# Layer-norm statistics of a four-layer graph kernel: two rows read by one statistics instruction

## The reference

```python
def _layernorm(x, axis=-1, eps=1e-05):
    m = jnp.mean(x, axis=axis, keepdims=True)
    v = jnp.var(x, axis=axis, keepdims=True)
    return (x - m) / jnp.sqrt(v + eps)

x = _layernorm(x + _L0_gnn_ref(...), axis=-1)
x = _layernorm(x + _L1_gnn_ref(...), axis=-1)
x = _layernorm(x + _L2_gnn_ref(...), axis=-1)
x = _layernorm(x + _L3_gnn_ref(...), axis=-1)
```

## Time and profile before

| | |
|---|---|
| median of 3 runs | 1827.29 us (1821.63 to 1827.8) |
| the profiled execution | 1824.94 us |
| its span, first to last instruction | 1822.8 us |
| PE, DVE, ACT, POOL busy | 1447.3, 1518.1, 1085.2, 1221.6 us |
| mean granted clock of TensorE | 0.923 |
| statistics instructions (L660) | 1,800, of 276 to 281 ns |

### The profile page before, as it was taken

One profiled execution on the slowest core, in us unless ns is written; L12 is line 12 of the kernel. 1 busy time (PEld: TensorE's weight loads), 2 busy tenths in 40 slices (PEclk: granted clock), 3 DMA queues, 4 the chain that ended last, 5 costly groups with the idle time before them and its releaser, 6 DMA issues.

```text
span 1822.8 us, 24302 instructions
## 1 busy us (share of the span) xinstructions
PE 1447.3 (79%) x6228; PEld 920.3 (50%) x6228; DVE 1518.1 (83%) x4392; ACT 1085.2 (60%) x2688; POOL 1221.6 (67%) x910
## 2 busy tenths in 40 slices
PE   2677777777787737877888499999898499999995
PEld 1344444444454425666666355555555255555552
DVE  3999999999999947999999589999999366666663
ACT  0467777777777754999999735655555233333331
POOL 7467666666766737888883188877772557777764
PEclk8789989899989878999999789999999799999998
DMA  5334444444444335676675445455442333443320
GB/s 145 84 79 100 100 105 105 93 101 97 96 107 105 62 94 126 180 189 181 187 189 159 126 111 128 124 132 138 130 107 76 100 88 88 98 98 90 88 75 21
DMA packets 165804, 205.15 MB, mean 113 GB/s; under 512 B 66823, under 2 KB 97918, under 8 KB 165666
## 3 DMA queue, kind: packets, MB, share of 16 engines
q1 hardware_dynamic: 108066, 179.45, 37.3%
q0 software_dynamic: 57600, 24.15, 7.5%
HBM read 147.12 MB, written 70.80 MB: 120 GB/s over the span
## 4 chain that ended last, share of the span: by engine, by line
DVE 59%; PE 27%; issue 8%; ACT 3%; DMA 1%; SPq 1%; POOL 0%; DVEq 0%; POOLq 0%; ACTq 0%
PE po L1210 16%; DVE bst L660 16%; DVE masked L866 5%; DVE run L738 5%; DVE po L707 4%; DVE sel L709 4%; DVE y L703 3%; DVE po L706 3%; DVE y L698 2%; PE pt L1195 2%; PE po L1205 2%; PE pb L1433 2%; PE pa L1474 1%; PE pc L1474 1%; PE pb L1474 1%
## 5 line engine op out<-in xcount | busy, mean ns | idle before, releaser
L475 POOL DMA_INDIRECT xs<-target_rows,slot_all x276 | 385.7, 1397 | 235.4 <-DMA xs<-source_rows 156.1
L951 ACT ACTIVATE x<-y,nmr,rst 125x128 f32<-125x128 f32 x800 | 322.7, 481 | 47.5 <-DVE nmr L688 47.5
L1210 PE MATMUL po<-wnt,rt 128*125 128x384 f32 x800 | 311.6, 538 | 0.6 <-ACT rt L988 0.6
L475 POOL DMA_INDIRECT xs<-in_x,src_all x100 | 148.1, 1481 | 136.2 <-issue 136.2
L1210 PEld LDWEIGHTS po<-wnt,rt 128*125 128x125 f32 x800 | 172.9, 216 | 117.0 <-issue 40.2
L1205 PE MATMUL po<-ball,ones_bf 128*125 128x512 bf16 (+1 forms) x512 | 153.2, 429 | 80.5 <-DVE sel L709 76.5
L1195 PE MATMUL pt<-ident,x 125*128 125x125 f32 x800 | 125.1, 280 | 99.5 <-issue 73.1
L1210 PE MATMUL po<-wnt,run 128*125 128x384 f32 x600 | 201.5, 486 | 0.0
L482 POOL DMA_INDIRECT out_rows<-do,last_all x100 | 121.5, 1215 | 89.9 <-ACT do L951 48.4
L660 DVE BATCH_NORM_STATS2 bst<-y 125x6 f32<-125x128 f32 x800 | 164.8, 278 | 3.8
L951 ACT ACTIVATE do<-yd,nmr,rst 125x128 f32<-125x128 f32 x400 | 163.6, 482 | 6.6 <-DVE nmr L688 6.6
(11 more groups left out here) (188 smaller groups left out, 3150.0 us busy)
## 6 DMA issues: line engine op xcount, KB each, us to landing
xin<-in_x SPq DMA_DIRECT2D x100, 224.0 KB
out_rows<-res SPq DMA_DIRECT2D x100, 224.0 KB
same<-same_d SPq DMA_DIRECT2D x75, 250.0 KB, 4.0
source_rows<-so SPq DMA_DIRECT2D x75, 224.0 KB
target_rows<-do SPq DMA_DIRECT2D x75, 224.0 KB
xs<-source_rows SPq DMA_DIRECT2D x69, 224.0 KB
xd<-target_rows SPq DMA_DIRECT2D x59, 224.0 KB
rel<-in_etype SPq DMA_DIRECT2D x50, 250.0 KB, 4.7
```

Source lines behind the costliest of these rows:

```text
L475: return nc.gpsimd.indirect_dma_start(out=to, out_offset=None, in_=table, in_offset=bass.IndirectOffsetOnAxis(ap=index, axis=0), bounds_ch ...
L951: last = A(to[:, j, :], y[:, j, :], ACT.Identity, scale=rst[s][:, k:k + 1], bias=nmr[s][:, k:k + 1])
L1210: last = mm(po[0:R, j * 512:j * 512 + NT * D], left(j), wnt[:, k, :, :].rearrange("k t d -> k (t d)"), start=False, stop=stop, skip_group_ ...
```

## The change

A statistics instruction now reads two rows of a partition at once, with their elements alternating: element 0 of row j, element 0 of row j+1, element 1 of row j, and so on, 256 elements. Its even half is then row j and its odd half is row j+1, each complete, so the sums that joined halves are left out. The table of statistics has three numbers a row, where it had six. The epsilon terms are added by operations with two tensor inputs, the second a constant held in memory (floors), and the copy in edge_rows1 is written as a maximum of a tensor with itself. The mean is read from the table with its own stride.

```diff
-        bst = two(sb, "bst", [R, G * T, 6])
-        msum, mdif, ve, seed, rst, nmr, tmp = (two(sb, n, [R, G * T]) for n in
-                                                   ("msum", "mdif", "ve", "seed", "rst", "nmr", "tmp"))
+        bst = two(sb, "bst", [R, G * T, 3])
+        floors = sb("floors", [R, 2])
+        ve, seed, rst, nmr, tmp = (two(sb, n, [R, G * T]) for n in ("ve", "seed", "rst", "nmr", "tmp"))
...
+            V.memset(floors[:, 0:1], D * EPS * EPS)
+            V.memset(floors[:, 1:2], D * EPS)
...
             def stats(y, s, g):
-                for j in range(T):
-                    last = V.bn_stats(bst[s][:, g * T + j, :], y[:, j, :])
+                for j in range(0, T, 2):
+                    to = bst[s][:, g * T + j:g * T + j + 2, :].rearrange("p j k -> p (j k)")
+                    last = V.bn_stats(to, y[:, j:j + 2, :].rearrange("p j d -> p d j"))
                 return last
 
             def variances(s, n, twice):
-                g, both = slice(0, n * T), twice * T
-                b_, ms, md, v, q = (a[s] for a in (bst, msum, mdif, ve, tmp))
-                V.tensor_tensor(md[:, g], b_[:, g, 1], b_[:, g, 4], ALU.subtract)
-                V.tensor_tensor(ms[:, g], b_[:, g, 1], b_[:, g, 4], ALU.add)
-                step(V.tensor_tensor(v[:, g], b_[:, g, 2], b_[:, g, 5], ALU.add))
-                step(V.scalar_tensor_tensor(out=q[:, g], in0=md[:, g], scalar=D / 4.0, in1=md[:, g], op0=ALU.mult, op1=ALU.mult))
-                step(V.tensor_tensor(v[:, g], v[:, g], q[:, g], ALU.add))
+                both = twice * T
+                v, m2 = ve[s], bst[s][:, :, 2]
                 if twice:
-                    last = V.tensor_scalar(v[:, 0:both], v[:, 0:both], 1.0 + EPS, D * EPS * EPS, ALU.mult, ALU.add)
+                    last = V.scalar_tensor_tensor(out=v[:, 0:both], in0=m2[:, 0:both], scalar=1.0 + EPS,
+                                                  in1=floors[:, 0:1].broadcast_to([R, both]), op0=ALU.mult, op1=ALU.add)
                 if n > twice:
-                    last = V.tensor_scalar(v[:, both:n * T], v[:, both:n * T], D * EPS, None, ALU.add)
+                    last = V.tensor_tensor(v[:, both:n * T], m2[:, both:n * T],
+                                           floors[:, 1:2].broadcast_to([R, n * T - both]), ALU.add)
                 last.then_inc(s_var, 1)
...
-                V.scalar_tensor_tensor(out=m[:, g], in0=ms[:, g], scalar=-0.5, in1=r[:, g],
+                V.scalar_tensor_tensor(out=m[:, g], in0=b_[:, g, 1], scalar=-1.0, in1=r[:, g],
                                        op0=ALU.mult, op1=ALU.mult).then_inc(done, 1)
...
-                return V.tensor_copy(bst[s][:, T:2 * T, :], bst[s][:, 4 * T:5 * T, :])
+                edge = bst[s][:, 4 * T:5 * T, :]
+                return V.tensor_tensor(bst[s][:, T:2 * T, :], edge, edge, ALU.max)
```

More of the change, by code:

```diff
@@ L682, in scales @@
                 g = slice(0, n * T)
-                ms, v, e, r, t, m = (a[s] for a in (msum, ve, seed, rst, tmp, nmr))
+                b_, v, e, r, t, m = (a[s] for a in (bst, ve, seed, rst, tmp, nmr))
                 dve.wait_ge(s_seed, next(seeds))
```

## The result

The changed kernel takes **1759.91 us** in the median of 4 runs (1757.07 to 1762.81), the kernel before on the same chip 1824.55: a ratio of 0.9645, with a 95% interval of 0.9618 to 0.9673. The forecast was 1758 us. The profiled execution took 1757.07 us, its span 1755.0. One execution of all that follow, of the changed kernel measured again, ran in a slower state of the chip (1789.30 us, granted clock 0.887) and is left out of its ratio.

What follows compares the result with a forecast made beforehand. DVE was taken to bound layers 0 to 2 and PE layer 3. Terms of -20, -19, -23 and -5 us sum to -67, from 1824.9 us profiled to 1757.9; forecast 1758 us, range 1725 to 1865.

Steps and rivals of the forecast that it cites:

- The price of the read: Statistics on DVE: one alternating 256-element read costs 328 ns against 388 for a pair, 60 ns saved; other end +130.
- the dear rival: The alternating read in the statistics runs at 1.79 ns an element, so the kernel gets slower, 1863 us; chance 0.22.
- The small sums: DVE's short instructions between statistics and scan: 0.92 us a chunk saved in layer 0, 1.10 in layer 1, 0.80 in layer 2.
- Layer 0: DVE saves 1.88 us a chunk, but a loop through PE and ACT lets 0.85 count: 24 times, -20 us.
- Layer 1: DVE saves 1.70 us a chunk; ACT is late next, chunk put at 11.98 us: 24 x 0.8, -19 us.
- Layer 2: DVE saves 1.28 us a chunk; PE is late next, 0.95 of its 1.05 us slack taken: 24 times, -23 us.
- Layer 3: PE is busy the whole time and covers DVE's saving: 0.
- Passages: Six dense-only blocks between layers, first chunks and last rows, latency chains of about 1 us each: -5 us.
- The sum: Whole kernel: -20 - 19 - 23 - 5 = -67 us, giving 1757.9 from the profiled execution, 1760 from the median.
- a middling price: The read costs 1.5 to 1.7 ns an element, the sums pay for it, time near 1825 us; chance 0.08.
- hidden after all: Loops in layers 0 and 2 take back nearly all, only layer 1 and chains gain: about 1793 us; chance 0.08.
- the four chances: Full rate as summed (1725 to 1785) 0.62, hidden after all 0.08, middling 0.08, dear read 0.22, of which 0.06 beyond 1865.

Runs made afterwards that it cites:

- e2: The changed kernel with each 256-element statistics read taking both rows in turn, but in steps of 16 words within a row: 1841.55 us, ratio 1.0091.
- e8: The changed kernel with only the first two rows of each tile measured by statistics instructions: 1749.14 us, ratio 0.9586.
- e6: The changed kernel without the 100 slot lookups that POOL issues mostly during layer 1: 1747.53 us, ratio 0.9579.
- e7: The kernel before the change, with the same POOL slot lookups left out: 1821.78 us, ratio 0.9983.
- e11: The changed kernel with slot lookups of eight chunks issued ahead of layer 1 and none in chunks 2, 6 and 10: 1748.40 us, ratio 0.9580.
- e9: The changed kernel with slot lookups of eight chunks instead of five issued before layer 1's row gathers: 1753.91 us, ratio 0.9615.
- e1: The changed kernel with each 256-element statistics instruction reading its two rows one after the other instead of alternating: 1756.19 us, ratio 0.9610.
- e5: The changed kernel with one-input epsilon terms and a plain tensor copy in layer 1 again: 1759.69 us, ratio 0.9648.

## Why the prediction was right

- **The price of the read** was the open question, and the end that was taken is the one measured: a saving of 53 ns a pair against 60 forecast and +130 for the dear rival. The reason given (neighbouring words within four elements) is borne out by e2, which costs 1.75 ns an element and loses to the kernel before. The dear rival was put down with 0.22 and a time of 1863; it was a real danger, an order of elements away.
- **The small sums**: 0.18 us remain in layer 0 (0.19 forecast), and in layer 2 from L671 at 1166.25 to the masks at 1166.41 0.16 (0.19). In layer 1 from the copy at 783.07 to the scan at 783.45 it is 0.38 (0.40).
- **Layer 0**: -26 against -20. The mechanism is right: DVE waits before L685 for ACT and before L703 for PE, and e8 shows that this loop is the whole limit now, at 22.7 us. In a usual chunk the size is right as well. Before and after:

```profile
279.24 1.89 PE L1205 MATMUL po<-ball,ones_bf 128*125 128x512 bf16 x4 [3.30 <-DVE sel L709]
284.43 1.04 PE L1268 MATMUL po<-wab,xt 128*125 128x128 f32 x8
293.09 0.16 DVE L685 SCALAR_TENSOR_TENSOR tmp<-seed 125x32 f32<-125x32 f32 x1
...
271.75 1.08 PE L1206 MATMUL po<-ball,ones_bf 128*125 128x512 bf16 x4 [2.46 <-DVE sel L709]
276.94 1.04 PE L1269 MATMUL po<-wab,xt 128*125 128x128 f32 x8
284.77 0.19 DVE L685 SCALAR_TENSOR_TENSOR tmp<-seed 125x32 f32<-125x32 f32 x1 [0.42 <-ACT seed L961]
```

  The products take 6.23 us in both (5.95 in the chunk of the prediction). From their end to L685 it was 7.62 us and is 6.79, where the forecast had 7.74 and 7.0. The next such products start after 24.53 us before and after 23.69 now: 0.84 us less, and the sum had 0.85. What the sum left out is how TensorE's clock changes from chunk to chunk. In four of the last 20 chunks before, the products took 7.4 us (328.10 to 335.52, granted clock 0.60; 0.73 in the usual chunk), and the chunk 25.6. The changed kernel has no such chunk, but four others in which the products run at the full clock and take 4.53 us:

```profile
295.44 1.08 PE L1206 MATMUL po<-ball,ones_bf 128*125 128x512 bf16 x4 [2.47 <-DVE sel L709]
296.35 2.74 PE L1211 MATMUL po<-wnt,rt 128*125 128x384 f32 x8
298.93 1.04 PE L1269 MATMUL po<-wab,xt 128*125 128x128 f32 x8
```

  By the starts of L747 the last 20 periods fell from 24.69 to 23.53 us on average, and the first four, of which the sum made no case of their own, by 2.8 us together. So of the 26 us some 17 are the 0.84 of the usual chunk, some 3 the first four chunks, and 6 are left over for these changes of the clock, which I had held fixed. That split is read from the starts; no run tested it.
- **Layer 1**: -8 against -19. This is the step that failed: "DVE would need 12.78 - 1.70 = 11.08 us, but ACT is busy 89.8% of 12.78 = 11.47 us" took ACT for the next bound and read POOL's 219 of 300 us as slack. The price of the chunk came out for as long as POOL had its lead (11.96 us in the first 15 periods), and wrong for the rest (13.24). With its issue time POOL stood at 89%, and at a pace of 11.98 it would have needed over 100% while it issues eight gathers a chunk. e6, e7, and e11 beside e9, show it.
- **Layer 2**: -27 against -23. PE's idle time before the transposes of L1448 is gone, and PE is at 99%. The sum had 12.86 us of PE's work and 0.10 of slack in a chunk; measured are 99.0% of 12.77 = 12.65 and 0.12. So the work was put 0.2 us too high, and why it shrank was not looked into. **Layer 3**: unchanged at 14.30 us and 100% PE. **Passages**: -6.4 against -5.
- **The sum** was nearer than its terms: +11 us in layer 1 were made up by -6, -4 and -1 elsewhere. That the total is off by only 2 us is luck, and overstates what the prediction knew.
- The other rivals: a middling price (e1: the read is free within 5 ns) and "hidden after all" (1793 us) are both out, though the second has its grain of truth: behind the sums, the statistics part adds 19 of its 38 us.
- **Figures that do not follow from their own terms**: at 598 ns a pair the three layers add 59 + 24 + 21 us, less 1 for the chains, so +103 and 1928 us, where the prediction says +110 and 1935. In the lower end of 1725, layer 1 gives 22 us; at ACT's 11.47 us a chunk it would be 24 x 1.31 = 31, and the end 1716. And the four chances add up to 1 without the 0.06 that is said to lie below the range. None of this touches the forecast of 1758.

## What to carry to other kernels

Price short instructions by their pitch in a run, not by their duration: the page's 278 ns for a statistics instruction was 194 of DVE's time, and a pair at 2 x 278 against one of 419 would have been put at a saving of 137 ns, where 53 are saved. When an engine that paced everything gets faster, go through every other engine's load at the new pace, queue by queue, and count the issue time behind each DMA instruction of POOL as POOL's own: a "78% busy" engine was the bound of layer 1. Look at the period along the layer as well as on average: a lead can hide such a bound for the first half of the chunks, and the mean of 12.44 us hides 11.96 early and 13.24 late here. And let one instruction with even and odd halves read two rows in turn where the rows are contiguous; the same read with hops inside a row costs half as much again.

## What the runs showed of the hardware

- One statistics instruction over 256 float32 elements has a pitch of 330 ns contiguous, 335 ns alternating between two rows 512 bytes apart, and 507 ns when each row is walked in steps of 64 bytes; two of 128 elements take 388 ns. The alternation as nearly free was to me only the likelier case.
- The same group of TensorE products takes 4.48 us in layer 0 where it follows other work without idle time, and mostly 5.9 to 6.2 us where it follows idle time, of 3.3 us before and of 2.5 in the changed kernel; the granted clock is 1.00 over the first and 0.73 over a group of 6.2 us. In four of 19 such places of the changed kernel it took 4.53 us at the full clock after the same 2.5 us.
- After an indirect DMA instruction of POOL 0.30 us or more pass before the next one starts, on top of its own 1.2 us or more. The profile does not count that as busy.
- One-source copies and scalar operations of 4 to 24 columns take up to 0.66 us while POOL issues indirect DMAs, the two-source operations that replace them at most 0.23. Of the kernel before's 212 (L673, L675, L842), 64 took over 0.3 us, and each of these ended 2 to 31 ns before an indirect DMA instruction of POOL did; in e5 it is the same for all 52. One of them, with POOL's instruction:

```profile
807.80 0.66 DVE L673 TENSOR_SCALAR ve<-ve 125x8 f32<-125x8 f32 x1
...
807.20 1.28 POOL L475 DMA_INDIRECT xdb<-target_rows,slot_all  x1 [0.31 <-issue]
```

  The median durations (170 ns) hide it; the means show it (369 and 502 ns). What it costs in time was not settled: the medians of e5 show nothing, layer 1 of its profiled execution some 3 us.
